# Score masks behind all products, unpadded 128-column products and a reordered ScalarE queue in an attention kernel

## The chip, the cores and the metric

The kernel runs on one core of a Trainium2 chip. The metric is device time in microseconds (us) for the whole program; lower is better. The core has a matrix engine (TensorE, PE in the profile), VectorE (DVE), ScalarE (ACT), GpSimd (POOL) and SyncE (SP, which here only issues DMAs). Each runs its own list of instructions in order; semaphores connect them.

## The reference

The program is one transformer layer: a layer norm, a sparse attention, a residual sum, then a second norm and a feed-forward part for the tokens picked by a router. The change touches the attention alone. Cut to what matters (8 sequences of 512 tokens, 16 heads of 128):

```python
q = _rope((x @ Wq)); k = _rope((x @ Wk)); v = x @ Wv     # per head
s_cmp = q @ k_block_mean.T * scale                       # 8 blocks of 64 keys
p_cmp = softmax(where(cmp_mask, s_cmp, -1e30))
s_full = q @ k.T * scale
p_slc = softmax(where(slc_mask, s_full, -1e30))          # causal
p_swa = softmax(where(swa_mask, s_full, -1e30))          # causal, last 64 keys
o = (p_cmp @ v_cmp) * g_cmp + (p_slc @ v) * g_slc + (p_swa @ v) * g_swa
return o @ Wo
```

Since a sequence has just 8 blocks and 8 are selected, the selected part is plain causal attention.

## The kernel before

The program has three parts: `normalise` (norm, transposed input `xt_hi`, `xt_lo`, gates), `attend`, and `project_and_route` (output product, router, feed-forward part).

`attend` works in 128 units, one for each head and sequence, numbered u = 8 x head + sequence. Every float32 product is made of three products of rounded parts (high x high, high x low, low x high) in the type F32R. It is software-pipelined by hand: in step u (the function `body`, written once for each engine) TensorE does, in this order,

1. the q and k projections of unit u (`project_one`, 12 products of 512 columns each, into banks 4 and 5);
2. the scores of unit u-1, in row tiles t = 0, 3, 2, 1 (list `SCORED`) into banks 0 to 3: three products of the tile's width and then a product `ident_h` x `causal_h` in bfloat16 that adds the causal mask to the diagonal block and raises `scores_ready`. Row tile t needs only (t+1) x 128 key columns, but the width is at least 256, so tile 0 is computed 256 wide. Before tile t's products it waits for `probs_ready`, that is, until unit u-2's probabilities have been mixed out of that bank;
3. ten transposes of the probabilities of unit u-2 (into banks 6, 7 and 4), after a wait for `v_lo_done`;
4. the v projection of unit u, four transposes of v of unit u-1, and the product of v and the transposed probabilities of unit u-2, key tiles j = 0 to 3, three products each. Key tile 3 needs the last 128 queries only; it is done 256 wide, with 128 columns of zeros in `pt_hi` and `pt_lo` (`PTQ0`, `PTOFF`, `PTW`).

VectorE reads each finished score tile (`read`: minimum, masked window with its minimum, block sums), subtracts the high parts of the transposed probabilities (`pt_low`), and, after ScalarE has done the exponentials, mixes the three softmaxes (`mix_far`, `mix_near`, `mix_window`) in the order t = 0, 3, 2, 1; `mix_window` raises `probs_ready`. Just ahead of the last one, `mix_window(v, 1)`, it computes `v_lo`. ScalarE evacuates projections (`evacuate`: q, k, v), rounds the high parts (`high`, `pt_high`) and computes the exponentials (`exp_of_row`, `exp_of_window`). GpSimd does the rotary embedding (`turn_cos`, `turn_sin`) and the low parts of q and k (`low`). SyncE issues the DMAs that swap the halves of q and k, store the output and load a head's weights (`Weights.load`) at the start of the step that is the last of the head before; ScalarE and GpSimd split those weights in the same step (`split`). The k projection of unit u+1 must wait until ScalarE has taken v of unit u out of bank 5 (`evacuated[2]`).

Of the kernel before, what the change touches and what calls it, by code (L numbers as in the profile page):

```python
# [6 lines left out]
B, N, D = 8, 512, 512  # L7
# [24 lines left out]
PTQ0 = [0, 128, 256, 256]  # L32
PTW = 1408
# [80 lines left out]
class Weights:  # L114
# [11 lines left out]
    def load(self, sp, h):  # L126
        for k in range(3):
            if not isinstance(h, int):
                sp.wait_ge(self.split[k], h * 2)
            sp.dma_start(self.raw[k][:], self.dram[k][:, :, bass.ds(h * HD, HD)]).then_inc(self.loaded[k], 16)  # L130
# [172 lines left out]
def attend(nc, phase, banks, m, gates, xt_hi, xt_lo, weights, rope_d, o_dram, chunks):  # L303
# [71 lines left out]


# [15 lines left out]
    with nc.Block() as block:  # L392
        @block.sync
        def _(sp):
# [6 lines left out]
            def body(u, b, project, score, end, split):  # L401
                if split is not False:
                    weights.load(sp, split)
# [13 lines left out]
            steps(sp, body, spare=load_chunks)  # L417
# [38 lines left out]
        def _(pe):  # L456
# [11 lines left out]
            def body(u, b, project, score, end, split):  # L468
# [8 lines left out]
                if score:  # L477

                    pe.wait_ge(lo_done[0], u)
                    pe.wait_ge(lo_done[1], u)  # L480
                    for t in SCORED:
                        w = max(256, (t + 1) * P)
# [3 lines left out]
                        for n, (x, v) in enumerate(((qk_hi[0], qk_hi[1]), (qk_hi[0], qk_lo[1]), (qk_lo[0], qk_hi[1]))):  # L486
                            nc.tensor.matmul(banks[t][:, 0:w], x[:, t * P:(t + 1) * P], v[:, 0:w], start=(n == 0), stop=(n == 2),  # L487
                                             skip_group_check=True)
                        nc.tensor.matmul(banks[t][:, t * P:(t + 1) * P], ident_h[:], causal_h[:], start=False, stop=True,  # L489
# [45 lines left out]
            pe.wait_ge(zeros_set, 5)  # L535
# [3 lines left out]
        def _(act):  # L539
# [18 lines left out]
            def pt_high(u, g):  # L558
                w = (512, 384, 384)[g]
                act.wait_ge(pt_ready, (u - 2) * 3 + g + 1)  # L560
                if g < 2:
                    nc.scalar.activation(pt_hi[:, PTOFF[g]:PTOFF[g] + w], banks[6 + g][:, 0:w], ACT.Copy).then_inc(pt_hi_done, 1)  # L562
                else:
                    nc.scalar.activation(pt_hi[:, PTOFF[2]:PTOFF[2] + 256], banks[4][:, 0:256], ACT.Copy)
                    nc.scalar.activation(pt_hi[:, PTW - P:PTW], banks[4][:, 256:384], ACT.Copy).then_inc(pt_hi_done, 1)
# [14 lines left out]
            def body(u, b, project, score, end, split):  # L580
# [5 lines left out]
                if end:  # L586
                    for g in range(3):
                        pt_high(u, g)
                if score:
# [3 lines left out]
                if project:  # L593
                    high(u, 0)
# [3 lines left out]
                if score:  # L598
                    exp_of_row(u, 1)
                    exp_of_window(u, 1)  # L600
# [4 lines left out]
                if project:  # L605
                    high(u, 1)
                if score:

                    act.wait_ge(cmp_step, (u - 1) * NC + 3)
                    nc.scalar.activation(sc, sc, ACT.Exp).then_inc(exp_cmp, 1)  # L610
                    exp_of_row(u, 0)
                    exp_of_window(u, 0)
# [8 lines left out]
        def _(dve):  # L621
# [11 lines left out]
            def pt_low(u, g):  # L633
                w = (512, 384, 384)[g]
                dve.wait_ge(pt_hi_done, (u - 2) * 3 + g + 1)
                if g < 2:
                    nc.vector.tensor_tensor(pt_lo[:, PTOFF[g]:PTOFF[g] + w], banks[6 + g][:, 0:w],
# [801 lines left out]
```

## Time and profile before

| | us |
|---|---|
| median of three runs | 2613.45 (2612.63 to 2614.03) |
| the profiled execution, own time | 2615.07 |
| its span, first to last instruction | 2613.2 |
| of it `attend` (from 102 to 1992) | 1890.0 |
| PE, DVE, ACT, POOL busy, share of the span | 95%, 70%, 54%, 61% |

A busy time is the sum of records. TensorE's matmuls overlap and the profile models their ends, so the distance from one start to the next says more than a record's duration, and a PE that is 95% busy may still be waiting. "Idle before" names what ended an engine's wait.

### The profile page before, as it was taken

The page shows a single profiled execution, that of the slowest core. Times are in us where ns is not written, and L with a number is a line of the kernel's source. Part 1 is how long each engine was busy: PE and PEld are TensorE (multiplying, and loading weights), DVE is VectorE, ACT ScalarE, POOL GpSimd, SP SyncE. Part 2 cuts the span into 40 slices and gives each one's busy share as a digit, 9 for nine tenths or more (in the row PEclk, how much of TensorE's full clock was granted, in tenths as well). Part 3 has the DMA queues.
Part 4 walks back from the last instruction along what each step waited for, and adds up shares of the span by engine and source line. Part 5 has one row for each costly group of instructions (what it writes and reads, how often), then busy time and mean ns, then how long its engine had stood idle before and what let it go on. Part 6 is the DMA issues. An engine that isn't in the chain of part 4 may idle for free. (4 is left out here: it accounts for less than half of the span.)

```text
span 2613.2 us, 48889 instructions
## 1 busy us (share of the span) xinstructions
PE 2488.2 (95%) x12944; PEld 2065.2 (79%) x12944; DVE 1840.7 (70%) x6021; ACT 1413.8 (54%) x3938; POOL 1598.5 (61%) x1177
## 2 busy tenths in 40 slices
PE   4799999999999999999999999999996999999998
PEld 3688888888888888888888888888885888887776
DVE  6387878787878787878777777777774466566134
ACT  6556666666666656565666666666663222222442
POOL 0377777676767777777777777777772434333442
PEclk9899999999999999999999999999997999999999
DMA  3122212121212222222221212121213443342356
GB/s 118 52 56 65 69 51 70 50 71 49 72 48 72 60 60 60 60 60 60 60 71 49 72 48 72 49 71 49 70 50 140 154 144 112 128 145 69 97 172 214
DMA packets 145629, 211.74 MB, mean 81 GB/s; under 512 B 14912, under 2 KB 56128, under 8 KB 144576
## 3 DMA queue, kind: packets, MB, share of 16 engines
q1 hardware_dynamic: 145600, 211.37, 27.3%
q8 instruction: 16, 0.26, 0.0%
q14 instruction: 13, 0.11, 0.0%
HBM read 93.87 MB, written 50.33 MB: 55 GB/s over the span
## 5 line engine op out<-in xcount | busy, mean ns | idle before, releaser
L463 PE MATMUL bank<-xt_hi,w_hi 128*128 (+1 forms) x1536 | 613.0, 399 | 4.5 <-DVE causal_h L728 3.7
L463 PE MATMUL bank<-xt_lo,w_hi 128*128 (+1 forms) x1536 | 601.2, 391 | 0.0
L463 PE MATMUL bank<-xt_hi,w_lo 128*128 (+1 forms) x1536 | 600.6, 391 | 0.0
L436 POOL TENSOR_TENSOR qk_lo<-s_full,qk_hi 128x512 fp32r<-128x512 f32 x256 | 330.4, 1293 | 257.9 <-ACT qk_hi L556 257.6
L424 POOL TENSOR_TENSOR cosed<-s_full,rope 128x512 f32<-128x512 f32 x256 | 329.1, 1289 | 178.3 <-ACT s_full L545 178.2
L432 POOL TENSOR_TENSOR s_full<-cosed,s_swap 128x512 f32<-128x512 f32 x256 | 329.4, 1287 | 36.7
L463 PEld LDWEIGHTS bank<-xt_hi,w_lo 128*128 128x128 f32 x1536 | 289.1, 188 | 63.2
L463 PEld LDWEIGHTS bank<-xt_hi,w_hi 128*128 128x128 f32 x1536 | 289.3, 188 | 58.1 <-DVE causal_h L728 4.0
L571 ACT ACTIVATE bank<-bank,shift 128x512 f32<-128x512 f32 (+3 forms) x512 | 262.4, 512 | 134.2 <-DVE bank L631 134.2
L463 PEld LDWEIGHTS bank<-xt_lo,w_hi 128*128 128x128 f32 x1536 | 289.7, 189 | 52.1
L429 POOL TENSOR_TENSOR s_swap<-s_swap,rope 128x512 f32<-128x512 f32 x256 | 330.4, 1291 | 0.0
L562 ACT ACTIVATE pt_hi<-bank 128x512 fp32r<-128x512 f32 (+1 forms) x256 | 125.5, 543 | 331.4 <-PE bank L502 331.4
L785 POOL TENSOR_TENSOR o_lo<-o_raw,o_hi 128x2048 fp32r<-128x2048 f32 x32 | 147.2, 4600 | 253.8 <-ACT o_hi L896 204.5
L545 ACT ACTIVATE s_full<-bank 128x512 f32<-128x512 f32 x256 | 156.0, 609 | 214.8 <-PE bank L463 213.5
L627 DVE TENSOR_REDUCE shift<-bank 128x1 f32<-128x512 f32 (+3 forms) x512 | 246.0, 481 | 20.4 <-PE bank L489 20.3
L631 DVE TENSOR_REDUCE bank<-bank 128x8 f32<-128x512 f32 (+3 forms) x512 | 252.6, 493 | 0.0
L487 PE MATMUL bank<-qk_hi,qk_hi 128*128 128x256 f32 (+2 forms) x512 | 200.2, 391 | 37.4 <-DVE probs L666 36.6
L693 DVE TENSOR_REDUCE sums<-bank 128x4 f32<-128x32 f32 x128 | 24.6, 192 | 297.9 <-ACT bank L571 297.9
L577 ACT ACTIVATE win<-win,shift 128x192 f32<-128x192 f32 (+1 forms) x512 | 230.8, 451 | 0.0
L958 PE MATMUL bank<-wo_hi,o_hi 128*128 128x512 f32 x512 | 204.9, 400 | 6.5 <-PEq L392 3.3
L650 DVE SCALAR_TENSOR_TENSOR bank<-bank,coef,cb 128x192 f32<-128x192 f32 (+1 forms) x512 | 206.1, 403 | 0.0
L958 PE MATMUL bank<-wo_hi,o_lo 128*128 128x512 f32 x512 | 200.3, 391 | 0.0
(170 smaller groups left out, 5831.4 us busy)
## 6 DMA issues: line engine op xcount, KB each, us to landing
s_swap<-s_full SPq DMA_DIRECT2D x512, 128.0 KB, 2.3
o_scratch<-o_sb SPq DMA_DIRECT2D x128, 256.0 KB, 2.0
o_raw<-o_scratch SPq DMA_DIRECT2D x32, 1024.0 KB, 6.2
xin<-in_L_attn_x SPq DMA_DIRECT2D x16, 1024.0 KB, 5.3
w_raw<-in_L_ffn_W SPq DMA_DIRECT2D x64, 256.0 KB, 3.2
base_scratch<-x SPq DMA_DIRECT2D x8, 1024.0 KB, 4.7
base<-base_scratch SPq DMA_DIRECT2D x32, 256.0 KB, 4.2
out<-base SPq DMA_DIRECT2D x32, 256.0 KB, 2.7
```

Source lines behind the costliest of these rows:

```text
L424: nc.gpsimd.tensor_tensor(cosed[k][:], s_full[k][:], rope[:, 0, :], ALU.mult).then_inc(cos_done[k], 1)
L429: nc.gpsimd.tensor_tensor(s_swap[k][:], s_swap[k][:], rope[:, 1, :], ALU.mult).then_inc(sin_done[k], 1)
L432: nc.gpsimd.tensor_tensor(s_full[k][:], cosed[k][:], s_swap[k][:], ALU.add).then_inc(roped[k], 1)
L436: nc.gpsimd.tensor_tensor(qk_lo[k][:], s_full[k][:], f32(qk_hi[k][:]), ALU.subtract).then_inc(lo_done[k], 1)
L463: last = nc.tensor.matmul(banks[QB[k]][:, :], w[k][:, c, :], v[:, bass.ds(b, 1), c, :], start=(n == 0), stop=(n == 3 * C - 1))
L487: nc.tensor.matmul(banks[t][:, 0:w], x[:, t * P:(t + 1) * P], v[:, 0:w], start=(n == 0), stop=(n == 2), skip_group_check=True)
L571: nc.scalar.activation(n, n, ACT.Exp, bias=shift1[:, t:t + 1], scale=-1.0, accum_out=sums[:, 1, t:t + 1]).then_inc(exp_row, 1)
L577: nc.scalar.activation(win[:, t, lo:], win[:, t, lo:], ACT.Exp, bias=shift2[:, t:t + 1], scale=-1.0, accum_out=sums[:, 2, t:t + 1]).then_i ...
L627: nc.vector.tensor_reduce(shift1[:, t:t + 1], n[:, 0:(t + 1) * P], AX.X, ALU.min)
L631: nc.vector.reduce_sum(sc[:, t, 0:nb], n[:, 0:nb * BS].rearrange("p (n s) -> p n s", s=BS), AX.X).then_inc(row_read, 1)
L650: return nc.vector.scalar_tensor_tensor(out=to.rearrange("p (n s) -> p n s", s=BS), in0=e, scalar=coef[:, 1, t:t + 1], in1=cb[:, t, b0:b1] ...
L958: last = nc.tensor.matmul(banks[t][:, :], o[k % 2][:, g, t * P:(t + 1) * P], w[:, k * G + g, :], start=(k == 0 and n == 0), stop=(k == K - ...
```

## The change

- Masks: all twelve score products of a unit come first, and the four mask products follow behind them in a second loop over `SCORED`. `scores_ready` rises with the masks, so no tile is ready before the last tile's products are issued.
- Padding: tile 0 of the scores and key tile 3 of the output product become 128 columns wide. The zeroed columns go, and with them the two memsets; the third piece of `pt_high` and of `pt_low` becomes one instruction of 384 columns instead of 256 + 128.
- ScalarE's order: `high(u, 0)` moves ahead of the exponentials of tiles 3 and 2, `high(u, 1)` ahead of those of tile 1, and the evacuation of v and of the output move behind all exponentials.
- VectorE's order: `v_lo` moves behind `mix_window(v, 1)`.
- SyncE: the weights of head h+1 are loaded in the first step of head h, about seven units before they are split.
- TensorE waits for the constants (`zeros_set`) only ahead of the first scores.

```diff
@@ consts
-PTQ0 = [0, 128, 256, 256]
-PTW = 1408
+PTQ0 = [0, 128, 256, 384]
+PTW = 1280
@@ sync
-            def body(u, b, project, score, end, split):
-                if split is not False:
-                    weights.load(sp, split)
+            def body(u, b, project, score, end):
...
+            def head_from_second(first, second, h):
+
+                body(first, B - 1, True, True, True)
+                body(second, 0, True, True, True)
+                if not (isinstance(h, int) and h == H - 1):
+                    weights.load(sp, h + 1)
+                with sp.Fori(1, B - 1) as b:
+                    body(h * B + b, b, True, True, True)
...
+            body(0, 0, True, False, False)
+            body(1, 1, True, True, False)
+            weights.load(sp, 1)
...
+            with sp.Fori(1, H - 1) as h:
+                head_from_second(h * B - 1, h * B, h)
@@ tensor
                 if score:
 
+                    if not end:
+                        pe.wait_ge(zeros_set, 3)
                     pe.wait_ge(lo_done[0], u)
                     pe.wait_ge(lo_done[1], u)
                     for t in SCORED:
-                        w = max(256, (t + 1) * P)
+                        w = (t + 1) * P
                         if end:
 
                             pe.wait_ge(probs_ready, (u - 2) * T + mixed_at[t])
                         for n, (x, v) in enumerate(((qk_hi[0], qk_hi[1]), (qk_hi[0], qk_lo[1]), (qk_lo[0], qk_hi[1]))):
                             nc.tensor.matmul(banks[t][:, 0:w], x[:, t * P:(t + 1) * P], v[:, 0:w], start=(n == 0), stop=(n == 2),
                                              skip_group_check=True)
+                    for t in SCORED:
                         nc.tensor.matmul(banks[t][:, t * P:(t + 1) * P], ident_h[:], causal_h[:], start=False, stop=True,
                                          skip_group_check=True).then_inc(scores_ready, 1)
...
-            pe.wait_ge(zeros_set, 5)
             steps(pe, body, start)
@@ scalar, pt_high (pt_low on VectorE alike)
-                if g < 2:
-                    nc.scalar.activation(pt_hi[:, PTOFF[g]:PTOFF[g] + w], banks[6 + g][:, 0:w], ACT.Copy).then_inc(pt_hi_done, 1)
-                else:
-                    nc.scalar.activation(pt_hi[:, PTOFF[2]:PTOFF[2] + 256], banks[4][:, 0:256], ACT.Copy)
-                    nc.scalar.activation(pt_hi[:, PTW - P:PTW], banks[4][:, 256:384], ACT.Copy).then_inc(pt_hi_done, 1)
+                nc.scalar.activation(pt_hi[:, PTOFF[g]:PTOFF[g] + w], banks[(6, 7, 4)[g]][:, 0:w], ACT.Copy).then_inc(pt_hi_done, 1)
@@ scalar, body
+                if project:
+                    high(u, 0)
                 if score:
                     for t in (3, 2):
                         exp_of_row(u, t)
                         exp_of_window(u, t)
                 if project:
-                    high(u, 0)
+                    high(u, 1)
+                if score:
+                    exp_of_row(u, 1)
+                    exp_of_window(u, 1)
+                    act.wait_ge(cmp_step, (u - 1) * NC + 3)
+                    nc.scalar.activation(sc, sc, ACT.Exp).then_inc(exp_cmp, 1)
+                    exp_of_row(u, 0)
+                    exp_of_window(u, 0)
+                if project:
                     if score:
                         act.wait_ge(v_transposed, u)
                     evacuate(u, 2)
-                if score:
-                    exp_of_row(u, 1)
-                    exp_of_window(u, 1)
                 if end:
...
-                if project:
-                    high(u, 1)
                 if score:
-
-                    act.wait_ge(cmp_step, (u - 1) * NC + 3)
-                    nc.scalar.activation(sc, sc, ACT.Exp).then_inc(exp_cmp, 1)
-                    exp_of_row(u, 0)
-                    exp_of_window(u, 0)
                     act.wait_ge(v_transposed, u)
                     nc.scalar.activation(v_hi[:].rearrange("p t d -> p (t d)"), banks[7][:, :], ACT.Copy).then_inc(v_hi_done, 1)
@@ vector, body
                     mix_near(1)
+                    mix_window(v, 1)
                     dve.wait_ge(v_hi_done, v + 1)
                     nc.vector.tensor_tensor(v_lo[:].rearrange("p t d -> p (t d)"), banks[7][:, :],
                                             f32(v_hi[:].rearrange("p t d -> p (t d)")), ALU.subtract).then_inc(v_lo_done, 1)
-                    mix_window(v, 1)
...
-            nc.vector.memset(f32(pt_hi[:, PTOFF[3]:PTOFF[3] + P]), 0.0).then_inc(zeros_set, 1)
-            nc.vector.memset(f32(pt_lo[:, PTOFF[3]:PTOFF[3] + P]), 0.0).then_inc(zeros_set, 1)
```

On TensorE, where the scores of a unit stand between its k projection and the transposes of the probabilities, the list before reads (numbers in `qk_hi_897` are buffers: 896 and 898 are k, 897 and 899 are q):

```order
L487 MATMUL bank<-qk_hi_897,qk_hi_896 128x256
L487 MATMUL bank<-qk_lo_899,qk_hi_896 128x256
L487 MATMUL bank<-qk_hi_897,qk_lo_898 128x256
L489 MATMUL bank<-causal_h,ident_h 128x128
L485 REGISTER_ALU
L487 MATMUL bank<-qk_hi_897,qk_hi_896 128x512
L487 MATMUL bank<-qk_lo_899,qk_hi_896 128x512
L487 MATMUL bank<-qk_hi_897,qk_lo_898 128x512
L489 MATMUL bank<-causal_h,ident_h 128x128
```

The same place in the changed list, from tile 2's first product to the transposes:

```order
L505 MATMUL bank<-qk_hi_897,qk_hi_896 128x384
L505 MATMUL bank<-qk_lo_899,qk_hi_896 128x384
L505 MATMUL bank<-qk_hi_897,qk_lo_898 128x384
L503 REGISTER_ALU
L505 MATMUL bank<-qk_hi_897,qk_hi_896 128x256
L505 MATMUL bank<-qk_lo_899,qk_hi_896 128x256
L505 MATMUL bank<-qk_hi_897,qk_lo_898 128x256
L508 MATMUL bank<-causal_h,ident_h 128x128 x4
L512 REGISTER_ALU
L521 MATMUL bank<-misc,probs 128x128 x10
```

The masks no longer stand between the float32 products; four of them stand in a row.

On ScalarE, from the exponentials of tile 2 to the end of a step (`sums` is the row sum that an exponential leaves), before:

```order
L577 ACTIVATE win,sums<-win,shift_913 128x192
L555 REGISTER_ALU
L556 ACTIVATE qk_hi_896<-s_full_892 128x512
L545 ACTIVATE vt<-bank 128x512
L569 REGISTER_ALU
L571 ACTIVATE bank,sums<-bank,shift_912 128x256
L577 ACTIVATE win,sums<-win,shift_913 128x192
L603 ISA
L604 ACTIVATE o_sb<-bank 128x512
L556 ACTIVATE qk_hi_897<-s_full_893 128x512
L609 ISA
L610 ACTIVATE bank<-bank 128x32
```

And in the changed list, from the same exponential to the copy of the output:

```order
L591 ACTIVATE win,sums<-win,shift_913 128x192
L574 ACTIVATE qk_hi_897<-s_full_893 128x512
L583 REGISTER_ALU
L585 ACTIVATE bank,sums<-bank,shift_912 128x256
L591 ACTIVATE win,sums<-win,shift_913 128x192
L614 ISA
L615 ACTIVATE bank<-bank 128x32
L583 REGISTER_ALU
L585 ACTIVATE bank,sums<-bank,shift_912 128x128
L591 ACTIVATE win,sums<-win,shift_913 128x128
L563 ACTIVATE vt<-bank 128x512
L625 ACTIVATE o_sb<-bank 128x512
```

Three copies of 512 columns (`qk_hi_896`, `vt`, `o_sb`) have left the stretch between the exponentials of tile 2 and those of tile 0.

## Rows read from the trace of the kernel before

**Rows 1.** `attend`: us, busy PE, PEld, DVE, ACT, POOL (count), granted clock, DMA.
```profile
102.00:1992.00 1890.00, 1838.19 (x9984) 1534.43 (x9984) 1476.63 (x5253) 1169.81 (x3632) 1368.57 (x1072) 0.99 0.23 61
```
**Rows 2.** Timeline of PE, one unit's scores: start, us taken, instruction.
```profile
1005.21 0.28 PE L487 MATMUL bank<-qk_lo,qk_hi 128*128 128x256 f32 x1
1005.33 0.28 PE L487 MATMUL bank<-qk_hi,qk_lo 128*128 128x256 f32 x1
1005.45 0.23 PE L489 MATMUL bank<-causal_h,ident_h 128*128 128x128 bf16 x1
1005.49 0.47 PE L487 MATMUL bank<-qk_hi,qk_hi 128*128 128x512 f32 x1
1005.80 0.39 PE L487 MATMUL bank<-qk_lo,qk_hi 128*128 128x512 f32 x1
1006.03 0.40 PE L487 MATMUL bank<-qk_hi,qk_lo 128*128 128x512 f32 x1
...
1006.92 0.23 PE L489 MATMUL bank<-causal_h,ident_h 128*128 128x128 bf16 x1
1007.39 0.39 PE L487 MATMUL bank<-qk_hi,qk_hi 128*128 128x256 f32 x1 [0.25 <-DVE probs L666]
...
1007.86 0.23 PE L489 MATMUL bank<-causal_h,ident_h 128*128 128x128 bf16 x1
1007.92 1.26 PE L502 MATMUL bank<-misc,probs 128*128 128x128 f32 x10
```
**Rows 3.** Timeline of PE, the same mask product one unit later.
```profile
1020.00 0.23 PE L489 MATMUL bank<-causal_h,ident_h 128*128 128x128 bf16 x1
```
**Rows 4.** Timeline of DVE from the end of one unit's mixing.
```profile
1006.34 0.68 DVE L720 TENSOR_TENSOR v_lo<-bank,v_hi 128x512 fp32r<-128x512 f32 x1
1006.94 0.40 DVE L666 SCALAR_TENSOR_TENSOR probs<-win,coef,bank 128x192 f32<-128x192 f32 x1
1007.26 0.68 DVE L627 TENSOR_REDUCE shift<-bank 128x1 f32<-128x512 f32 x1
1008.13 0.69 DVE L631 TENSOR_REDUCE bank<-bank 128x8 f32<-128x512 f32 x1
1009.20 1.16 DVE L637 TENSOR_TENSOR pt_lo<-bank,pt_hi 128x512 fp32r<-128x512 f32 x2 [0.37 <-ACT pt_hi L562]
1016.68 0.19 DVE L693 TENSOR_REDUCE sums<-bank 128x4 f32<-128x32 f32 x1 [2.34 <-ACT bank L571]
```
**Rows 5.** Timeline of ACT in the same unit.
```profile
1008.57 0.98 ACT L562 ACTIVATE pt_hi<-bank 128x512 fp32r<-128x512 f32 x2 [2.67 <-PE bank L502]
1012.13 0.56 ACT L571 ACTIVATE bank<-bank,shift 128x384 f32<-128x384 f32 x1 [1.04 <-DVE bank L631]
1013.14 0.62 ACT L556 ACTIVATE qk_hi<-s_full 128x512 fp32r<-128x512 f32 x1
1013.66 0.59 ACT L545 ACTIVATE vt<-bank 128x512 f32<-128x512 f32 x1
1014.14 0.44 ACT L571 ACTIVATE bank<-bank,shift 128x256 f32<-128x256 f32 x1
1015.03 0.60 ACT L604 ACTIVATE o_sb<-bank 128x512 f32<-128x512 f32 x1
1015.51 0.64 ACT L556 ACTIVATE qk_hi<-s_full 128x512 fp32r<-128x512 f32 x1
1019.73 0.63 ACT L134 ACTIVATE w_hi<-w_raw 128x512 fp32r<-128x512 f32 x1 [1.80 <-DMA w_raw<-in_L_attn_Wq]
1020.27 0.58 ACT L545 ACTIVATE s_full<-bank 128x512 f32<-128x512 f32 x1
```
**Rows 6.** Groups of PE by form: count | busy us, mean ns | idle before.
```profile
L502 PE MATMUL bank<-misc,probs 128*128 128x128 f32 x1280 | 162.7, 275 | 7.3 <-DVE probs L666 7.3
```
**Rows 7.** Timeline of PE, plain float32 products of 128 columns.
```profile
2084.57 3.74 PE L992 MATMUL bank<-onehot,z 128*128 128x128 f32 x32
```
**Rows 8.** Timeline of PE, the first projection of `attend`.
```profile
102.48 0.79 PE L463 MATMUL bank<-xt_hi,w_hi 128*128 128x512 f32 x1 [3.74 <-DVE causal_h L728]
```

More of the change, by code:

```diff
@@ L127, in load @@
         for k in range(3):
-            if not isinstance(h, int):
+            if not (isinstance(h, int) and h == 0):
                 sp.wait_ge(self.split[k], h * 2)
@@ L415, in load_chunks @@
                 chunks.load_first(sp, 0)
-            steps(sp, body, spare=load_chunks)
+            def head_from_second(first, second, h):
[8 more added lines that the diff above has]
+            weights.load(sp, 1)
+            with sp.Fori(2, B - 1) as b:
+                body(b, b, True, True, True)
+            with sp.Fori(1, H - 1) as h:
+                head_from_second(h * B - 1, h * B, h)
+            head_from_second((H - 1) * B - 1, (H - 1) * B, H - 1)
+            body(H * B - 1, B - 1, True, True, True)
+            body(H * B, None, False, True, True)
+            load_chunks()
+            body(H * B + 1, None, False, False, True)
             sp.wait_ge(out_slot_free, 16 + 16 * H * B)
@@ L635, in pt_low @@
                 dve.wait_ge(pt_hi_done, (u - 2) * 3 + g + 1)
-                if g < 2:
-                    nc.vector.tensor_tensor(pt_lo[:, PTOFF[g]:PTOFF[g] + w], banks[6 + g][:, 0:w],
-                                            f32(pt_hi[:, PTOFF[g]:PTOFF[g] + w]), ALU.subtract).then_inc(pt_lo_done, 1)
-                else:
-                    nc.vector.tensor_tensor(pt_lo[:, PTOFF[2]:PTOFF[2] + 256], banks[4][:, 0:256],
-                                            f32(pt_hi[:, PTOFF[2]:PTOFF[2] + 256]), ALU.subtract)
-                    nc.vector.tensor_tensor(pt_lo[:, PTW - P:PTW], banks[4][:, 256:384],
-                                            f32(pt_hi[:, PTW - P:PTW]), ALU.subtract).then_inc(pt_lo_done, 1)
+                nc.vector.tensor_tensor(pt_lo[:, PTOFF[g]:PTOFF[g] + w], banks[(6, 7, 4)[g]][:, 0:w],
+                                        f32(pt_hi[:, PTOFF[g]:PTOFF[g] + w]), ALU.subtract).then_inc(pt_lo_done, 1)
             def mix(t, part, to):
@@ L728, in _ @@
             nc.vector.tensor_copy(causal_h[:], m("causal")).then_inc(zeros_set, 1)
-            dve.wait_ge(zeros_set, 5)
+            dve.wait_ge(zeros_set, 3)
             steps(dve, body, spare=lambda: chunks.low_wo(dve, 0))
```

## The prediction

> **What bounds the kernel now.** I read the busy times by stretch first. `attend` is 1890 us of the span, and PE is busy for 1838 of them [rows 1], at a granted clock of 0.99, so nearly all at the upper level of 2.4 GHz. That looks like a TensorE bound, but busy time is modelled, so I went to the timeline of one unit. The first mask product of a unit starts at 1005.45, the next unit's at 1020.00 [rows 2, 3]: a unit takes 14.55 us. Within it PE waits once. After the mask of tile 2 at 1006.92 the next product normally follows 0.04 us later (1005.45 to 1005.49), but here it starts at 1007.39, released by a `probs` write of DVE L666 [rows 2]. That stall is 0.47 - 0.04 = 0.43 us per unit, so PE's own list needs 14.55 - 0.43 = 14.12 us.
>
> So the bound is a loop through three engines. DVE's last mix ends at 1006.94 + 0.40 = 1007.34; call that point X [rows 4]. PE then does tile 1's products and starts the transposes at 1007.92 [rows 2]; ACT copies them from 1008.57 [rows 5]; DVE subtracts from 1009.20 and reads the other tiles; ACT waits 1.04 us for DVE's tile 2 and goes through its list; DVE waits 2.34 us for ACT's exponential of tile 0 [rows 4, 5] and then mixes again. This loop is 14.55 us long and PE has 0.43 to spare. Anything that PE saves alone is lost in that stall; anything that the loop saves is worth up to what PE's own list leaves.
>
> **The loop after the change.** Taken out of it, per unit:
> - `v_lo` no longer stands ahead of the last mix: 1006.94 - 1006.34 = 0.60 us [rows 4].
> - ACT's `vt` (1013.66 to 1014.14, 0.48) and `o_sb` (1015.03 to 1015.51, 0.48) go behind the exponentials [rows 5].
> - `high(u, 0)` (1013.14 to 1013.66, 0.52) goes ahead of the exponentials, where ACT had 1.04 us of waiting for DVE in the same stretch, which covers it [rows 5]. Without that cover it would cost its 0.52 again.
> - One 384-column piece for 256 + 128: under 0.1 us on each of ACT and DVE; I count 0.07.
>
> Together 2.15 us. Put in: `read(v, 3)` must now wait for a mask behind all products. From X, tile 1's first record starts 0.05 later and its mask place comes 1007.86 - 1007.39 = 0.47 after that; the second mask (tile 3's) some 0.07 later, its duration 0.23, the signal 0.05: X + 0.87. Before, `read` could start at 1007.26, before X. It takes until 1008.13 + 0.69 = 1008.82, that is 1.56 us, so `pt_low`, which is queued behind it, can start at X + 2.43 instead of 1009.20 = X + 1.86. The loop gains 0.57 us there. DVE spends 0.60 of this waiting time on `v_lo`, so that costs nothing more, and the transposes' wait for `v_lo_done` (X + 0.65) ends before the masks do. New loop: 14.55 - 2.15 + 0.57 = 12.97 us. PE's list of nearly 14 us is then longer, by about 1 us, and becomes the bound.
>
> **PE's list after the change**, from 14.12 us:
> - Masks. A mask between float32 products costs its own 0.04 and makes the product behind it 1005.80 - 1005.49 = 0.31 long instead of 1006.03 - 1005.80 = 0.23 [rows 2], so 0.12 us. Three such and the last (1007.86 to 1007.92, 0.06) make 0.42 to 0.46. No row shows one mask behind another. The bounds are 0.04 (start to start) and 0.12 (no gain at all); nearest is mask to transpose, 0.06, and I take 0.08, since a mask's own load is one more step. Four make 0.32, so 0.14 us saved (bounds 0 and 0.28).
> - Width 128 for 256, six products of the type F32R per unit. At 256 columns the step is 1005.33 - 1005.21 = 0.12 [rows 2]. No row has an F32R product of 128 columns. The transposes, also 128 wide with a 128-column float32 load each, step by (1.26 - 0.275) / 9 = 0.109 us [rows 2, 6]. The plain float32 products of 128 columns are two records each, 32 for 16 products, with (3.74 - 0.275) / 31 = 0.112 us a record, so 0.224 us a product [rows 7]. F32R products at 512 columns are one record of 0.23 us, not two, so I take the transposes' row: 0.01 less each at most, 0.03 us saved per unit. The other end is 6 x (0.224 - 0.118) = 0.64 us lost.
>
> The Trainium skill (TensorE: Matmul & The Clock Gate, section on LDWEIGHTS) puts a load at its columns over 1.2 GHz, 107 ns for 128. The transposes' 109 ns agree with it; by that figure the narrow products would save 0.06 us a unit at most, since the load binds below 256 columns.
>
> PE's list: 14.12 - 0.14 - 0.03 = 13.95 us, or 0.60 us less than a unit takes now. The stall and the masks appear in the 126 steps that have scores and mixing: 75.6 us.
>
> **What is given back.** `vt` leaves bank 5 later. On ACT's clock, tile 2's exponential now starts near X + 5.4 and `vt` ends near X + 9.2 (row and window of tile 2 1.0, `high` 0.52, tile 1 0.9, tile 0 0.8, `vt` 0.6). PE reaches the next k projection near X + 9.8. The margin of 0.6 us holds in ordinary units. In a head's last step ACT has two weight copies ahead of all this (1019.73 to 1020.27, 0.54 each [rows 5]), and the margin is gone by about 0.5 us: 15 x 0.5 = 7 us lost. The first unit's v evacuation and k rounding lie on the ramp: about 2 us. The weights a head ahead remove ACT's wait of 1.80 us on w_raw [rows 5], but the k evacuation behind it comes at 1020.27, only half a microsecond late, and no unit is longer for it: nothing now. `zeros_set`: PE's first projection was released by DVE's last constant [rows 8]; DVE needs well under 1 us for five small constants, so I count nothing.
>
> **Sum.** 75.6 - 7 - 2 = 67 us. The profiled execution took 2615.07 (span 2613.2), the median is 1.6 lower; against the median 2613.45 - 67 = 2546 us. With the masks at their bounds it is 2564 and 2528 us.
>
> **Rivals.**
> - A: an F32R product of 128 columns runs like a plain float32 one, 0.224 us. For it: the plain products show a float32 type with just this price at just this width [rows 7], and no F32R product in the trace is narrower than 256. Against it: the one-record pace at 512, 384 and 256 columns falls in proportion to the width. PE's list is then 13.95 + 0.03 + 0.64 = 14.62 us, 0.07 over today's unit: 126 x 0.07 = 9 us lost, the gain of the stall is eaten. About 2621 us, slower. It decides from a step of about 0.21 us per product on. Chance 0.13.
> - B: the change doesn't free PE: a wait on ACT takes the stall's place. The candidate is bank 5: if ACT's list is 0.3 us per unit later than I count, the margin of 0.6 is used up through unit-to-unit variation and weight steps, and PE waits at the k projection for some 0.3 us: 38 us of the 67 are gone, 2584 us. For it: POOL and ACT both gain work in a head's last step, and POOL's list of 8 x 1.29 us plus three weight parts comes close to a 13.95 us unit. Against it: POOL has over 3 us free in every other unit. Chance 0.12.
> - C: a 128-column product steps faster than the transposes, down to the mask's 0.06. Then 6 x (0.118 - 0.06) = 0.35 us instead of 0.03, 40 us more, 2506 us. The same page of the Trainium skill (Back-to-back issue gap) states about 81 ns for a sustained load and product of 128 columns. By it the gain would be 0.22 us a unit, but the transposes do not go below 109 ns in this trace. Chance 0.04.
>
> **How the numbers follow.** My case has 0.70, with its own range 2530 to 2565; A 0.13, B 0.12, C 0.04, the rest 0.01. The range reaches over my case and B, 2530 to 2600, about 0.8. A measurement of this kernel can tell 0.2% (5 us) from no change: faster is my case, B and C and little of A's spread, 0.86; A's spread of some 15 us around +8 gives within 0.2% 0.04 and slower 0.10.
>
> **What the profile of the changed kernel would show.** Mask starts of neighbouring units 13.9 to 14.0 us apart (A: 14.6; B: 14.2 to 14.3). No wait of PE for DVE `probs` ahead of tile 1; DVE waiting at `read(v, 3)` for the masks instead, and less than 1 us at `sums` for ACT. Steps between the 128-column products of about 0.11 us. In each head's last unit a PE wait for `vt`. The prediction is wrong if the 128-column step is over 0.15 us, if four masks in a row cost as much as four apart, or if PE waits in ordinary units for `vt`.

## The result, and the profile after

The changed kernel takes 2586.94 us in the median (2585.36 to 2588.58), the kernel before beside it 2613.74: a ratio of 0.9896 with a 95% interval of [0.9885, 0.9908], so 1.0% faster. That is inside the predicted range, but the gain is 27 us where 67 were forecast. The figure comes close to that of the prediction's rival B (2584), and by accident: the loss has another cause, as shown below. The profiled execution took 2585.80 us, with a span of 2584.0.

The ordinary unit first. Timeline of PE in the changed kernel, one unit's scores and the mask groups one unit before and after it (start, us taken, instruction; "x4" is a run of four):

```profile
993.99 0.40 PE L508 MATMUL bank<-causal_h,ident_h 128*128 128x128 bf16 x4
...
1005.90 0.22 PE L505 MATMUL bank<-qk_hi,qk_hi 128*128 128x128 f32 x1
1005.95 0.28 PE L505 MATMUL bank<-qk_lo,qk_hi 128*128 128x128 f32 x1
1006.07 0.27 PE L505 MATMUL bank<-qk_hi,qk_lo 128*128 128x128 f32 x1
1006.18 0.44 PE L505 MATMUL bank<-qk_hi,qk_hi 128*128 128x512 f32 x1
...
1007.69 0.29 PE L505 MATMUL bank<-qk_hi,qk_lo 128*128 128x256 f32 x1
1007.82 0.40 PE L508 MATMUL bank<-causal_h,ident_h 128*128 128x128 bf16 x4
1008.05 1.26 PE L521 MATMUL bank<-misc,probs 128*128 128x128 f32 x10
...
1022.43 0.40 PE L508 MATMUL bank<-causal_h,ident_h 128*128 128x128 bf16 x4
```

From 993.99 to 1007.82 the unit takes 13.83 us, against 14.55 before [rows 2, 3]; 13.95 was forecast. PE has no wait between the products any more (before it waited for `probs` ahead of tile 1 [rows 2]), and the products of 128 columns follow each other by 0.12 and 0.11 us (1005.95 to 1006.07 to 1006.18). The four masks take 1008.05 - 1007.82 = 0.23 us in all. The next unit, to 1022.43, takes 14.61: it is the last step of a head.

The units of before are 14.51 to 14.56 us, 14.54 in the mean, so 125 units times 0.71 should give 88 us. (`attend` has 127 distances from one unit's masks to the next one's; the first two are ramp.) The waits between 400 and 1930 us say where most of it went (engine, what waits, for whom: us in total, times, longest):

```profile
ACT qk_hi L574 <- POOL s_full L448: 138.4, 107, 4.0
DVE shift L641 <- PE bank L508: 115.1, 107, 2.2
POOL s_swap L445 <- DMA s_swap<-s_full: 33.5, 12, 3.1
PE bank L479 <- ACT vt L563: 30.0, 25, 2.4
```

The last two lines are new. PE waits for `vt` 25 times, twice a head, and GpSimd waits for the swap of q 12 times, once a head. The longer of the two stalls of a head begins on SyncE. SyncE's queue some 10 us further on, from the output store of a head's first step to q's swap of the next step:

```profile
1031.82 0.34 SPq L405 DMA_DIRECT2D o_scratch<-o_sb  x1
1032.43 0.41 SPq L130 DMA_DIRECT2D w_raw<-in_L_attn_Wq  x1
1032.94 0.50 SPq L130 DMA_DIRECT2D w_raw<-in_L_attn_Wk  x1
1033.53 0.45 SPq L130 DMA_DIRECT2D w_raw<-in_L_attn_Wv  x1
1034.18 0.47 SPq L396 DMA_DIRECT2D s_swap<-s_full  x1
1034.70 0.59 SPq L397 DMA_DIRECT2D s_swap<-s_full  x1
```

Three weight loads of 256 KB stand between the store and the two halves of q's swap. What then happens on GpSimd, ScalarE and TensorE, each in a line or two of its timeline (in square brackets the idle time ahead, and what ended it):

```profile
1039.35 1.29 POOL L445 TENSOR_TENSOR s_swap<-s_swap,rope 128x512 f32<-128x512 f32 x1 [2.84 <-DMA s_swap<-s_full]
```
```profile
1042.19 0.63 ACT L574 ACTIVATE qk_hi<-s_full 128x512 fp32r<-128x512 f32 x1 [3.68 <-POOL s_full L448]
...
1047.04 0.60 ACT L563 ACTIVATE vt<-bank 128x512 f32<-128x512 f32 x1
```
```profile
1047.69 0.50 PE L479 MATMUL bank<-xt_hi,w_hi 128*128 x1 [2.08 <-ACT vt L563]
...
1049.07 0.63 PE L479 MATMUL bank<-xt_lo,w_hi 128*128 x1
1049.50 0.63 PE L479 MATMUL bank<-xt_hi,w_lo 128*128 x1
```

The swap's second half is issued at 1034.70 and GpSimd can go on only at 1039.35, 4.65 us later, where a swap of this kernel lands in 2.3 us in the median. `high(u, 0)` waits for GpSimd in every unit now, 0.8 us in an ordinary one, which costs nothing there; here the wait is longer. `high(u, 0)` now stands ahead of the exponentials, so ScalarE waits 3.68 us for it, everything behind it in ScalarE's list is late, `vt` last of all, and PE stands still for 2.08 us. The busy times by stretch show the DMA and what the stall does to TensorE's clock (stretch, its length, busy us and count of PE, PEld, DVE, ACT and POOL, granted clock, DMA share, GB/s):

```profile
1033.00:1039.00 6.00, 6.00 (x40) 5.33 (x39) 5.07 (x14) 1.96 (x4) 2.28 (x2) 1.00 0.90 236
1039.00:1047.50 8.50, 6.62 (x35) 5.35 (x33) 4.51 (x20) 5.31 (x20) 7.60 (x6) 1.00 0.01 4
1047.50:1052.00 4.50, 4.31 (x12) 3.43 (x13) 4.43 (x16) 1.60 (x4) 1.27 (x1) 0.62 0.41 117
```

Behind the stall the granted clock of the stretch is 0.62, a mix of the levels of 1.2 and 2.4 GHz, and a projection product steps by 0.43 us (1049.07 to 1049.50) instead of 0.23. Such a stretch of 3.4 us at the lower level follows the stall in eight heads. This unit is 17.8 us long (masks at 1036.27 and 1054.09); the fourteen of its kind are 15.5 to 18.1 us, together 44.7 us above 13.83. The eight with such a stretch are 17.6 to 18.1 us, PE's wait and 1.9 us more than 13.83; the six without it are 15.5 to 16.5 us, PE's wait and 0.3 us more. So some 8 x 1.55 = 12 us of the 44.7 are the lower clock's.

The shorter stall is in a head's last step. GpSimd first, then ScalarE and TensorE in the same unit:

```profile
1005.38 1.29 POOL L138 TENSOR_TENSOR w_lo<-w_raw,w_hi 128x512 fp32r<-128x512 f32 x1
...
1008.02 1.28 POOL L138 TENSOR_TENSOR w_lo<-w_raw,w_hi 128x512 fp32r<-128x512 f32 x1
```
```profile
1012.12 0.63 ACT L574 ACTIVATE qk_hi<-s_full 128x512 fp32r<-128x512 f32 x1 [2.06 <-POOL s_full L448]
```
```profile
1017.62 0.50 PE L479 MATMUL bank<-xt_hi,w_hi 128*128 x1 [0.45 <-ACT vt L563]
```

GpSimd computes `w_lo` of q and k ahead of the turns that `high(u, 0)` waits for. These fifteen units are 14.6 us long, 11.5 us in all. The first two units of `attend` take 17.12 + 13.83 us where they took 11.34 + 14.88, 4.7 us more. The account: 88 - 44.7 - 11.5 - 4.7 = 27, against a span that is 29.2 us shorter; most of the other 2 us lie behind `attend`'s last masks (646.5 us instead of 648.3).

### The profile page after: what moved, and what is told of

Read it like the earlier page. It is cut to its first block and busy times, and to the rows that moved or that the text cites. A ratio compares the mean times of both kernels' runs of the same rounds, so it can differ in the third digit from the quotient of the medians.

```text
span 2584.0 us, 48592 instructions
## 1 busy us (share of the span) xinstructions
PE 2453.7 (95%) x12944; PEld 2082.9 (81%) x12944; DVE 1843.8 (71%) x5891; ACT 1412.9 (55%) x3810; POOL 1590.1 (62%) x1177
## 5 line engine op out<-in xcount | busy, mean ns | idle before, releaser
L479 PE MATMUL bank<-xt_hi,w_hi 128*128 (+1 forms) x1536 | 630.4, 410 | 43.8 <-ACT vt L563 40.0
L479 PE MATMUL bank<-xt_hi,w_lo 128*128 (+1 forms) x1536 | 607.6, 396 | 0.0
L452 POOL TENSOR_TENSOR qk_lo<-s_full,qk_hi 128x512 fp32r<-128x512 f32 x256 | 324.8, 1291 | 0.3 <-ACT qk_hi L574 0.3
L579 ACT ACTIVATE pt_hi<-bank 128x384 fp32r<-128x384 f32 (+1 forms) x384 | 174.6, 528 | 250.2 <-PE bank L521 250.2
L574 ACT ACTIVATE qk_hi<-s_full 128x512 fp32r<-128x512 f32 x256 | 160.4, 626 | 171.9 <-POOL s_full L448 171.9
L585 ACT ACTIVATE bank<-bank,shift 128x512 f32<-128x512 f32 (+3 forms) x512 | 251.3, 491 | 1.1 <-DVE bank L645 1.0
L591 ACT ACTIVATE win<-win,shift 128x192 f32<-128x192 f32 (+1 forms) x512 | 222.9, 435 | 0.0
L650 DVE TENSOR_TENSOR pt_lo<-bank,pt_hi 128x384 fp32r<-128x384 f32 (+1 forms) x384 | 206.2, 593 | 0.9 <-ACT pt_hi L579 0.8
L674 DVE SCALAR_TENSOR_TENSOR probs<-win,coef,bank 128x192 f32<-128x192 f32 (+1 forms) x512 | 199.9, 390 | 4.5
```

The lines of the kernel that those rows point to most:

```text
L452: nc.gpsimd.tensor_tensor(qk_lo[k][:], s_full[k][:], f32(qk_hi[k][:]), ALU.subtract).then_inc(lo_done[k], 1)
L479: last = nc.tensor.matmul(banks[QB[k]][:, :], w[k][:, c, :], v[:, bass.ds(b, 1), c, :], start=(n == 0), stop=(n == 3 * C - 1))
L585: nc.scalar.activation(n, n, ACT.Exp, bias=shift1[:, t:t + 1], scale=-1.0, accum_out=sums[:, 1, t:t + 1]).then_inc(exp_row, 1)
L591: nc.scalar.activation(win[:, t, lo:], win[:, t, lo:], ACT.Exp, bias=shift2[:, t:t + 1], scale=-1.0, accum_out=sums[:, 2, t:t + 1]).then_i ...
```

## The experiments

The profile gives an account, but not a cause: the clock, the sharing of the DMA engines and the place of the loads all change in the same units. The theory ("DMA") was: the loads cost 45 us because they stand ahead of q's swap in SyncE's queue. Its rivals: it is the split of the weights on ScalarE and GpSimd ("SPLIT"), or the clock by itself, whatever the loads do ("CLOCK").

**1. Where the loads stand.** In the first run they stay in the first step of the head, ahead of its store instead of behind it:

```diff
+                if load is not None:
+                    weights.load(sp, load)
                 if end:
                     (store of the output)
-                weights.load(sp, h + 1)      # behind the first step
+                body(second, 0, True, True, True, load=h + 1)
```

> The changed kernel, with one thing moved: in a head's first step SyncE issues the next head's three weight loads right behind the two swaps of that step instead of behind its output store, so that some 9 us without a swap follow. Theory DMA (the loads run into the q swap of the next step, GpSimd waits about 2.8 us for it, ScalarE's rounding of q and all exponentials behind it come late, and TensorE waits for vt in the next k projection): no unit over 15 us is left but the one of 14.6 in each head's last step; about 45 us faster than the changed kernel, 2542. Theory SPLIT (splitting the weights on ScalarE and GpSimd is what delays the units around a head's change): nothing changes, 2587. Theory CLOCK (TensorE's clock falls to its lower level by itself near a head's change and the long units follow from that): nothing changes, 2587, and the stretches at the lower level stay.

Measured: 2541.58 us, ratio to the kernel before 0.9714 [0.9698, 0.973]. SyncE's queue, and PE's only wait between 400 and 1870 us:

```profile
1001.85 0.60 SPq L397 DMA_DIRECT2D s_swap<-s_full  x1
1002.72 0.41 SPq L130 DMA_DIRECT2D w_raw<-in_L_attn_Wq  x1
1003.23 0.50 SPq L130 DMA_DIRECT2D w_raw<-in_L_attn_Wk  x1
1003.82 0.45 SPq L130 DMA_DIRECT2D w_raw<-in_L_attn_Wv  x1
1011.86 0.37 SPq L407 DMA_DIRECT2D o_scratch<-o_sb  x1
1012.69 0.47 SPq L396 DMA_DIRECT2D s_swap<-s_full  x1
```
```profile
PE bank L482 <- ACT vt L566: 5.7, 13, 0.4
```

The loads go out at 1002.72, behind k's swap and nine microseconds ahead of the store, and nothing else is issued between them and the store. The wait for the swap is gone, no stretch at the lower clock is left between the heads, and the long units are 13.8 us. Three loads moved ahead of one store are worth 45 us. The theory holds; the clock was a consequence of the stall.

**2. The loads at the place of the kernel before** (the last step of the head, ahead of the swaps; all else as changed):

```diff
-            if not (isinstance(h, int) and h == 0):
+            if not isinstance(h, int):
...
+                if split is not False:
+                    weights.load(sp, split)
                 if project:
                     swap(u, 0)
```

> The changed kernel with SyncE's list as it was before the change: a head's weights are loaded at the start of the step in which they are split. Theory DMA: the long unit after a head's first step goes, but ScalarE waits again for the load in the splitting step and, with vt now last in its list, TensorE waits longer there; estimate 0.5 to 3 us per head instead of 0.8 and about 4 in the changed kernel, so 2550 to 2575. Theory SPLIT: as the changed kernel or slower by ScalarE's wait, 2587 to 2615. Theory CLOCK: 2587.

Measured: 2590.45 us, 0.9913 [0.9897, 0.993]. That is above what "DMA" expected (2550 to 2575) and inside the range of "SPLIT" (2587 to 2615), but not for the reason of "SPLIT": the units behind a head's first step, which were 15.5 to 18.1 us long, are 13.8 now, and the loss has moved to another step. Waits between 400 and 1930 us:

```profile
ACT w_hi L134 <- DMA w_raw<-in_L_attn_Wq: 39.3, 13, 3.2
PE bank L461 <- ACT vt L545: 34.8, 13, 2.8
```

GpSimd no longer waits for the swap. The swap itself is late here too: the loads go out right ahead of it, as they did in the kernel before (there from 1016.84 on, q's halves at 1018.47 and 1018.99), and in both its halves land after 3.5 to 5.2 us. But in this step GpSimd has the low parts of q's and k's weights to compute ahead of the turns, and that covers the delay. What costs now is that the late weights hold up ScalarE, which waited for them before too, for 1.80 us [rows 5], and through ScalarE's rounding of them GpSimd. In the kernel before that cost nothing; in the new order of ScalarE, where `vt` is last, PE waits with it. The last steps of the heads are 16.6 to 19.3 us long, 58.6 us in all above 13.83, against 11.3 in run 1. Loads a head ahead are thus worth 49 us (2590.45 - 2541.58) in this order, and their place in the change took 45 of them back.

**3. GpSimd's list in the last step of a head.** `w_lo` of k goes behind the turns:

```diff
-                        if split is not False:
+                        if split is not False and k == 0:
                             weights.low(pool, nc.gpsimd, split, k)
...
+                    for k in range(2):
+                        turn_sin(u, k)
+                    if split is not False:
+                        weights.low(pool, nc.gpsimd, split, 1)
```

> The changed kernel, but in a head's last step GpSimd computes the low part of the k weights behind the two rotations instead of ahead of them. Theory DMA takes the 14.6 us unit to be a second, separate loss: GpSimd's 1.29 us for that part delays the rounded q, and so vt; moved, the unit of 14.6 becomes 13.9 to 14.1, about 8 to 11 us faster than the changed kernel, 2577, and the long units after a head's first step stay. Theory SPLIT: this part of the splitting carries the loss, so most of the 57 us at the heads' changes goes, 2540. Theory CLOCK: 2587.

Measured: 2567.16 us, 0.9817 [0.9801, 0.9833], 20 us below the changed kernel, where about 10 were expected. The 14.6 us units are 13.83: those 11 us had GpSimd's list as their cause. The other 9 or 10 lie in the long units (35.1 us above 13.83 instead of 44.7), where only two stretches at the lower clock are left of eight. The stalls themselves are as long as before (27.7 us of PE's wait in all, against 27.9); six fewer stretches at 1.55 us are the 9 us. What decides whether the clock falls behind a stall of some 2 us is not shown.

**4. The loads between the swap of q and the swap of k**, one step later:

```diff
                     swap(u, 0)
+                    if load is not None:
+                        weights.load(sp, load)
                     swap(u, 1)
```

> The changed kernel with the three weight loads issued one step later, between the q swap and the k swap. Theory DMA: the q swap is no longer behind the loads, the k swap is, but GpSimd comes to k only some 2.6 us after q, so that most of the delay is covered; the long units shrink from 15.5 to 18 us to 13.8 to 15, 2545 to 2560. If the sharing of the DMA engines, not the order of issue, were what delays q (its data still moves when the loads start about 1 us later), the loss stays near the changed kernel's, 2575 to 2587. Theories SPLIT and CLOCK: 2587.

Measured: 2558.04 us, 0.9784 [0.9768, 0.98]. The wait for the swap halves, and the long units are 14.1 to 15.6 us:

```profile
POOL s_swap L449 <- DMA s_swap<-s_full: 17.5, 12, 2.2
```

Now k's swap is the late one, and the list has more slack for it. The halves of q's swap, issued just ahead of the loads, land after 2.2 to 2.4 us in all fourteen heads, though the first load goes out 0.9 us behind the second of them (1020.59 after 1019.71); those of k's swap, issued behind the loads, take 3.7 to 5.1. So what counts is which transfer the loads stand ahead of, and (run 2) what its reader has to do meanwhile; sharing the DMA engines with loads that were issued later does not delay a swap here.

**5. Both repairs**, runs 1 and 3 together:

> The changed kernel with both edits: the weight loads ahead of the store, and the w_lo of k behind the sin and cos turns of s_full. If the two losses are separate (late loads in the step after the first of a head, GpSimd's w_lo at the last step of a head), they add: the first edit gave 45 us, the second 20 us as measured, of which about 11 lie in the last step itself; 2541.6 less 8 to 11 is 2531 to 2534. If the second edit only relieved the same wait that the first takes away, nothing is added: 2541. No unit should be longer than 14.1 us between the first and the last head.

Measured: 2533.24 us, 0.9686 [0.967, 0.9702]: 3.1% faster than the kernel before, and the fastest version. The busy times by stretch:

```profile
400.00:1870.00 1470.00, 1470.00 (x8287) 1275.54 (x8286) 1226.69 (x4253) 968.00 (x2905) 1126.83 (x888) 1.00 0.24 64
```

PE has no wait there, at the full clock. The two losses were separate and add as expected: this edit gives 8 us here (11 in the units; up to `attend`'s first masks this execution took 124.5 us instead of 121.7), and the other 9 of the 20 us of run 3 were the clock's share, which run 1 takes away already.

**6. The masks alone**, on the kernel before, to test the loop:

```diff
+                    for t in SCORED:
                         nc.tensor.matmul(banks[t][:, t * P:(t + 1) * P], ident_h[:], causal_h[:], ...
```

> The kernel before with one edit: the four causal masks of a unit behind all its score products, nothing else. By the loop PE, ACT, DVE that bounded the kernel before, the third read of the scores now waits for the masks, about 0.5 us a unit, and nothing else shortens the loop: 126 x 0.48 = 61 us slower, about 2675. By a count of PE's own work alone, where four masks in a row are cheaper than four apart (0.12 against 0.056 us each), it would be 126 x 0.25 = 32 us faster, about 2582.

Measured: 2676.27 us, 1.0233 [1.0216, 1.025]. The list of PE got shorter and the kernel 62 us slower. PE and DVE in one unit:

```profile
1005.38 0.39 PE L487 MATMUL bank<-qk_hi,qk_hi 128*128 128x256 f32 x1 [0.46 <-DVE probs L667]
...
1005.85 0.40 PE L490 MATMUL bank<-causal_h,ident_h 128*128 128x128 bf16 x4
...
1020.87 0.40 PE L490 MATMUL bank<-causal_h,ident_h 128*128 128x128 bf16 x4
```
```profile
1006.20 0.69 DVE L628 TENSOR_REDUCE shift<-bank 128x1 f32<-128x512 f32 x1 [0.87 <-PE bank L490]
```

PE still waits for `probs`, longer than before (0.46 us idle, 0.25 in [rows 2]), and DVE now waits for the masks ahead of its first read, that of tile 3. A unit is 15.03 us, 0.48 more than 14.55: the loop of the prediction, lengthened where it said, by 0.48 for its 0.57.

**7. `v_lo` alone** behind the last mix, on the kernel before:

```diff
+                    mix_window(v, 1)
                     dve.wait_ge(v_hi_done, v + 1)
                     (v_lo)
-                    mix_window(v, 1)
```

> The kernel before with one edit: v_lo of DVE behind the last mix of the unit. By the loop, 0.60 us leave it, and the loop then stands at 13.95, where PE's own list (14.12) becomes the bound: a gain of 0.3 to 0.43 us a unit, 38 to 54 us, 2561 to 2577. If DVE is not in the loop, nothing: 2615.

Measured: 2600.61 us, 0.9943 [0.9927, 0.996], a unit of 14.46: 13 us where I expected 38 to 54. DVE and PE:

```profile
1043.18 0.68 DVE L721 TENSOR_TENSOR v_lo<-bank,v_hi 128x512 fp32r<-128x512 f32 x1
```
```profile
1043.78 0.23 PE L489 MATMUL bank<-causal_h,ident_h 128*128 128x128 bf16 x1
1044.21 0.85 PE L502 MATMUL bank<-misc,probs 128*128 128x128 f32 x6 [0.20 <-issue]
```

The wait ahead of tile 1 is gone, but the transposes behind the last mask wait for `v_lo_done`: `v_lo` ends at 1043.86 and they start at 1044.21, where they otherwise follow a mask by 0.06 us. The profile itself says only "issue"; that this wait holds them is read from the code and the times (it is the last of their conditions to be met), and why they start as late as 0.35 us behind its end is not shown. The 0.60 us left one wait of the loop and came back in large part at the next. In the changed kernel the masks behind all products give `v_lo` the time (it ends at 1007.08, the transposes start at 1008.05), as the prediction's line on `v_lo_done` had it; my expectation for this run had forgotten it.

**8. ScalarE's order alone**, on the kernel before:

```diff
+                if project:
+                    high(u, 0)
                 (exponentials of tiles 3 and 2)
-                    high(u, 0)
-                    (evacuation of v)
+                    high(u, 1)
                 (exponentials of tile 1)
-                (evacuation of the output)
-                    high(u, 1)
                 (exponentials of the compressed branch and of tile 0)
+                (evacuation of v, then of the output)
```

> The kernel before with one edit: the order of ACT's copies in a unit as in the changed kernel. By the loop, 1.0 us and more leave it, so that PE's own list bounds: again 38 to 54 us, 2561 to 2577, less what PE then waits for vt in the last steps of the heads (up to 14 x 2.8 = 39 us, as where the loads stood at their old place in the changed kernel): up to 2610. If the order of ACT is of no account, 2615.

Measured: 2612.59 us, 0.9995 [0.9986, 1.0005], no change, and a little above the 2610 that had been expected at most. Behind that zero stand two large numbers. The last masks of two neighbouring units:

```profile
1009.59 0.23 PE L489 MATMUL bank<-causal_h,ident_h 128*128 128x128 bf16 x1
...
1023.65 0.23 PE L489 MATMUL bank<-causal_h,ident_h 128*128 128x128 bf16 x1
```

The unit is 14.06 us without any wait of PE, so this order alone takes the whole stall out and PE's list bounds. The other number is in the waits between 400 and 1930 us:

```profile
ACT w_hi L134 <- DMA w_raw<-in_L_attn_Wq: 35.5, 13, 2.9
PE bank L463 <- ACT vt L545: 28.2, 13, 2.3
```

125 x 0.48 = 60 us are gained, 53 are lost in the last steps of the heads (16.4 to 18.3 us long), 4 in the first two units, and the part behind `attend`'s last masks is 5 us longer, which no run explains. ScalarE's order needs the loads a head ahead.

**9 to 12. Masks and padding on PE's own list.** In the kernel of run 5 PE bounds every unit, so each edit of its list shows at full price. I ran masks behind or between, with and without the padding; the edits are the lines of the change itself, undone.

> The kernel of the last run but three (loads ahead of the store, w_lo of k later, 2533.2) with each mask again right behind its own tile's products. PE's own list bounds every unit there, so the price is that of four masks apart against four in a row: by the steps of the traces (0.12 against 0.056 to 0.067 with the first) 0.20 to 0.25 us a unit, 25 to 31 us, 2558 to 2564; by the step that the prediction took for a mask in a row (0.08), 0.14 us a unit, 18 us, 2551. If the masks' place has no price on PE and the loop bounds, it would be faster: 2533 or below.

> The same kernel (2533.2) with the score products of tile 0 again 256 columns wide, so that only the dropped padding is undone. By the steps of the trace (0.117 at 256 columns, 0.112 to 0.114 at 128) three products cost 0.01 to 0.02 us a unit more: 1 to 2 us, no difference that can be measured. If a product's time went by its columns, 0.06 us each: 0.17 us a unit, 22 us, 2555. If narrow F32R products ran at the rate of plain fp32, padding would make it faster by up to 0.3 us a unit.

> The kernel with the loads ahead of the store and w_lo of k later (2533.2), with all of the padding as in the kernel before (score products of tile 0, p times v of the last block row, two copies for the last group of the transposed probabilities) and the masks behind all products. If what the masks' move saves depends on the width of what stands around it (0.20 us a unit where all is padded, 0.14 where nothing is), a unit here is 13.86 us, 0.03 more than 13.83, as the prediction had it for the padding: 126 x 0.03 = 4 us, 2537. If the two savings simply add, the padding is worth 0.09 us, a unit is 13.92 and the time 2544.

> The same, with each mask right behind its own tile's products, so that PE's list is that of the kernel before, without its waits. PE's own list bounds: the unit of the run with ACT's order alone, 14.06 us, so 0.23 us a unit over 2533.2: 2562. By the list as the prediction worked it out (14.12) it would be 2570; if the loop through ACT and DVE still bounds without any wait to be seen, above 2570.

| | masks behind | masks between |
|---|---|---|
| nothing padded | 2533.24, unit 13.83 | 2549.59, unit 13.97 |
| score products of tile 0 padded | 2534.79, unit 13.84 | |
| all padded | 2536.62, unit 13.89 | 2558.34, unit 14.06 |

The ratios to the kernel before are 0.9757 [0.9742, 0.9772] (9), 0.9702 [0.9689, 0.9715] (10), 0.9684 [0.9668, 0.97] (11) and 0.9777 [0.9761, 0.9794] (12). The masks' move is worth 0.14 us a unit without padding and 0.17 with it; 0.20 to 0.25 had been expected for the first, which was too much. Run 11 came as expected; run 12 has the unit that was expected, and a time 4 us below the 2562. Dropping the padding is worth 0.05 us with the masks behind, of which the scores have 0.007. On the whole program the masks' move gives 16 us without padding and 22 with it: the units give 18 and 22, and what the ramps and the part behind `attend` add or take was not followed up. In run 9, where the masks stand between, PE's timeline shows why a mask is dear there:

```profile
1016.04 0.27 PE L511 MATMUL bank<-qk_hi,qk_lo 128*128 128x128 f32 x1
1016.16 0.23 PE L513 MATMUL bank<-causal_h,ident_h 128*128 128x128 bf16 x1
1016.20 0.47 PE L511 MATMUL bank<-qk_hi,qk_hi 128*128 128x512 f32 x1
1016.51 0.39 PE L511 MATMUL bank<-qk_lo,qk_hi 128*128 128x512 f32 x1
1016.74 0.40 PE L511 MATMUL bank<-qk_hi,qk_lo 128*128 128x512 f32 x1
```

The product behind a mask takes 0.31 us to its next (1016.20 to 1016.51), the one after it 0.23; behind a projection or another score product the same 512-column product takes 0.28 (1006.18 to 1006.46 in the changed kernel, behind a narrow one) or 0.23.

## Why the prediction came out as it did

- **The bound and the loop: right.** The loop PE, ACT, DVE with 0.43 us of slack on PE is shown by three runs: masks alone make it 0.48 us longer (0.57 forecast) and the kernel 62 us slower; ScalarE's order alone brings the unit to PE's own list; all of it together lets PE go without a wait. The signs came as forecast: in an ordinary unit DVE waits 1.09 us for the masks and 0.85 us at `sums`. The cover for `high(u, 0)` is in the trace too: tile 2's exponential starts at 984.85, when DVE has just read tile 2 (984.82). That the moves of `vt` and `o_sb` count in full was not measured one by one.
- **PE's own list: right in kind, 0.12 us too long.** The list of before is 14.06 us (runs 8 and 12), not 14.12. The masks and the padding save 0.175 + 0.052 = 0.23 us together (12 against 5), where the sum had 0.14 + 0.03. So the unit came to 13.83, and the term of 75.6 us measured 88.
- **The step that failed: "The weights a head ahead ... nothing now".** It looked at what the loads took away, ScalarE's wait of 1.80 us on `w_raw`, and not at what they were moved ahead of: q's swap in SyncE's queue, in a step in which GpSimd has nothing to do that covers a late swap (before, the loads delayed the q swap of a head's last step, behind GpSimd's work on the weights). Its lateness reaches PE by GpSimd, `high(u, 0)` and `vt`. That cost 44.7 us (27.9 us of PE's wait, some 12 us of lower clock behind it, the rest at PE's restart), and run 1 shows the cause, since moving the same loads ahead of one store gives it back. The term also took the wait that it removed to be free, which held in the old order of ScalarE and not in the new (runs 2 and 8).
- **The head's last step: right in place, too small, another cause.** 7 us were forecast and 11.5 measured. Not the weight copies on ScalarE make `vt` late, but `w_lo` on GpSimd ahead of the turns: run 3 moves only that, and these units are 13.83.
- **The first unit: 2 us forecast, 4.7 measured.** In the first step with scores `high(u, 0)` waits 4.1 us for GpSimd ahead of the first exponential, and PE waits 3.4 us for `vt` behind them. This was read from the trace and not tried. About 2.5 us of it are the clock's: in runs 9 and 12 PE waits as long there (3.3 and 3.2 us), no stretch at the lower level follows, and the first unit takes 14.6 us instead of 17.1; in the changed kernel the granted clock is 0.50 from 130.1 to 136.9 us.
- **The rivals.** A and C fall with the steps of 0.11 to 0.12 us at 128 columns and with run 10. B had the right kind of wait, PE at the k projection for `vt`, but put it in ordinary units through ScalarE's list: no ordinary unit has it. That its 2584 us is nearly the measured time is luck.

With all terms as measured, the sum would have been 88 - 45 - 11 - 5 = 27 us and the forecast 2586. The term of the loads alone, put at nothing, is larger than the whole miss of 40 us; the others partly cancel (12 us more from the units, 4 and 3 us less from the heads' last steps and the first units).

## What to carry to other kernels

When a load is moved earlier to take away a wait, look at what it is now ahead of in its queue, and follow that transfer to the engine that bounds: a place that is early enough and has nothing behind it (here ahead of the store, not behind it) was worth 45 us. When a list is reordered so that a step stands last, every wait that the list could afford before must be priced again. An edit that measures zero alone may be the half of a pair: ScalarE's order gave nothing without the loads, and the masks cost 62 us without ScalarE's order and `v_lo`, but are worth 16 us with them.

## What the runs showed of the hardware

- Four bf16 products of 128 columns in a row step by (0.40 - 0.23) / 3 = 0.057 us, and all four with their weight loads take 0.23 us (1007.82 to 1008.05). The Trainium skill (TensorE: Matmul & The Clock Gate, section "Wait — 56ns, not 53.3ns?") states 55.6 ns for this width at 2.4 GHz, and the trace agrees. The 81 ns that the same page of the Trainium skill (section "Back-to-back issue gap") gives for a load and product of 128 columns appear neither here nor in the float32 steps of 0.11 to 0.12.
- An F32R product of 128 columns steps by 0.11 to 0.12 us, like one of 256 (1007.57 to 1007.69), except the first of a run, whose next product follows after 0.05 (1005.90 to 1005.95). Halving the width of three products saved 0.007 us a unit (run 10 against run 5).
- Two halves of a swap that are issued 0.65 us behind three loads of 256 KB took 4.65 us until GpSimd could go on, where such a swap lands in 2.3 us alone. Halves issued ahead of such loads, the first of which follows 0.9 us later, land after 2.2 to 2.4 us (run 4).
- A PE stall of 1.9 to 2.4 us was followed in eight heads of the changed kernel by 3.4 us at the level of 1.2 GHz; in the other six, with stalls of 1.3 to 2.3 us, the level stayed. In run 3 two of fourteen such stalls were followed by it, and in run 1, where the stall is gone, no head has it.
